# Half of batch 1's first scores inside the values of batch 0, and projections between scores

## What is computed

```python
def _layernorm(x, axis=-1, eps=1e-05): ...      # mean, variance over the last axis

# attention: x (8, 256, 512), ctx (8, 256, 512), H = 32 query heads, G = 8 key groups, head width 16
q = X @ Wq.T + bq;  k = encoder_output @ Wk.T + bk;  v = encoder_output @ Wv.T + bv
scores = jnp.einsum('bgrqd,bgkd->bgrqk', q, k) / jnp.sqrt(jnp.float32(HD))
scores = jnp.where(causal_mask..., -jnp.inf, scores); scores = jnp.where(padding_mask..., -jnp.inf, scores)
w = jax.nn.softmax(scores, axis=-1)
out = jnp.einsum('bgrqk,bgkd->bgrqd', w, v)     # then out @ Wo.T + bo

# feed-forward (512 -> 2048 -> 512), weights rounded to -1, 0, 1, activations to 8 bits
bitlinear158(x, w, b) = act_quant(rms_norm(x)) @ weight_quant(w).T + b
h = jax.nn.silu(bitlinear158(x, w1, b1)); h = jax.nn.gelu(h, approximate=False)
h = layer_norm(h, ln_g, ln_b); ffn = bitlinear158(h, w2, b2)

x = x + attention(_layernorm(x), ctx);  x = x + ffn(_layernorm(x))
```

## Time and profile before

| | |
|---|---|
| median of 3 runs | 582.51 us (580.14 to 583.58) |
| profiled execution | 581.34 us, span 579.3 us |
| busy, of the span | PE 90%, PEld 49%, DVE 85%, ACT 61%, POOL 24% |
| granted clock of PE, mean | 0.964 of full speed |
| DMA | 72.17 MB, mean 125 GB/s |
| chain that ended last | PE 54%, DVE 20%, issue 8%, DMA 7%, ACT 7% |

### The profile page before, as it was taken

The page is one execution under the profiler, slowest core; times in us unless marked ns, Lnnn a source line. Parts: engine busy times, 40 slices in busy tenths (PEclk is TensorE's granted clock), DMA queues, the critical chain, the costliest instruction groups (busy, mean ns, idle before and its releaser), DMA issues.

```text
span 579.3 us, 9027 instructions
## 1 busy us (share of the span) xinstructions
PE 520.6 (90%) x3425; PEld 285.6 (49%) x3425; DVE 491.1 (85%) x730; ACT 351.4 (61%) x424; POOL 139.9 (24%) x106
## 2 busy tenths in 40 slices
PE   4978788999899999899999999999949999798796
PEld 3856335544564557445663566445514553243343
DVE  4689929789989788988999789978896889959996
ACT  2235470687848764785659573866368576876931
POOL 5103034003410621025200611211122105133130
PEclk9986899999899999999999999999969999988999
DMA  6888595887126712463137502571115411110002
GB/s 200 277 209 317 174 279 156 335 304 170 37 66 197 163 43 79 160 179 86 72 117 183 117 16 98 161 170 40 43 39 140 101 40 42 27 30 1 36 2 75
DMA packets 32994, 72.17 MB, mean 125 GB/s; under 512 B 7167, under 2 KB 14529, under 8 KB 29950
## 3 DMA queue, kind: packets, MB, share of 16 engines
q1 hardware_dynamic: 31286, 67.13, 39.6%
q0 software_dynamic: 576, 4.19, 1.8%
q10 hardware_dynamic: 1088, 0.24, 0.2%
HBM read 46.50 MB, written 20.61 MB: 116 GB/s over the span
## 4 chain that ended last, share of the span: by engine, by line
PE 54%; DVE 20%; issue 8%; DMA 7%; ACT 7%; POOL 2%; SPq 2%; ACTq 0%; DVEq 0%
PE FF L891 8%; PE FF L943 6%; DVE negm L1416 5%; PE S L773 5%; PE PV L813 5%; ACT PT L1136 5%; PE PV L830 4%; PE S L797 4%; PE FF L710 3%; DMA num<-o_raw 2%; PE PV L773 2%; PE FF L893 2%; DVE work L1565 2%; POOL st L510 2%; PE FF L905 2%
## 5 line engine op out<-in xcount | busy, mean ns | idle before, releaser
L1136 ACT ACTIVATE PT<-S 128x1024 f32<-128x1024 f32 x128 | 123.4, 1032 | 24.0 <-PE S L797 23.6
L1416 DVE TENSOR_REDUCE negm<-S 128x4 f32<-128x1024 f32 x88 | 105.6, 1215 | 17.9 <-PE S L773 16.5
L797 PE MATMUL S<-Q,K 100*128 100x512 bf16 x256 | 73.7, 393 | 18.6 <-ACT PT L1136 14.9
L891 PE MATMUL FF<-w1t,xqT 128*128 128x512 bf16 x256 | 68.4, 390 | 5.0 <-ACT wq_sb L1170 3.4
L813 PE MATMUL PV<-PT,vaug 128*32 128x256 f32 x1024 | 70.5, 394 | 0.6 <-ACT PT L1136 0.6
L773 PE MATMUL S<-K,Q 97*128 97x256 bf16 x352 | 55.5, 284 | 5.4 <-DVE negm L1416 3.5
L830 PE MATMUL PV<-wo_sb,num 128*128 128x512 f32 x128 | 59.1, 608 | 0.0
L1170 ACT ACTIVATE work<-FF,s 128x512 f32<-128x512 f32 x48 | 33.0, 687 | 36.3 <-PE FF L893 36.3
L1416 DVE TENSOR_REDUCE negm<-PV 128x4 f32<-128x1024 f32 x40 | 48.8, 1220 | 5.6 <-PE PV L773 5.2
L710 PE MATMUL FF<-xnT,wq_sb 128*128 128x256 f32 x224 | 50.6, 381 | 0.2 <-ACT xnT L1103 0.2
L1194 ACT ACTIVATE work<-work 128x2048 bf16<-128x2048 f32 x12 | 22.9, 1911 | 45.2 <-DVE work L1571 45.0
(11 more groups left out here) (231 smaller groups left out, 905.2 us busy)
## 6 DMA issues: line engine op xcount, KB each, us to landing
Q<-q_d SPq DMA_DIRECT2D x15, 768.0 KB
q_d<-part SPq DMA_DIRECT2D x8, 768.0 KB, 3.6
x_sb<-in_x SPq DMA_DIRECT2D x8, 512.0 KB, 4.1
ctx_sb<-in_ctxT SPq DMA_DIRECT2D x8, 512.0 KB, 4.6
work<-in_w SPq DMA_DIRECT2D x4, 1024.0 KB, 13.2
q_d<-part SPq DMA_DIRECT2D x8, 512.0 KB, 3.3
xb_sb<-in_x SPq DMA_DIRECT2D x8, 512.0 KB, 4.3
work<-in_w POOLq DMA_DIRECT2D x4, 1024.0 KB, 8.9
```

Of the source, the lines that this page charges most:

```text
L797: last = pe.matmul(where, K[0:ROWS_2, g, kt * P:(kt + 1) * P], Q[0:ROWS_2, g, 2 * pair:2 * pair + 2, :], start=not masked, stop=True)
L891: pe.matmul(FF[:, n % 2, :], xqT[:, k, t * P:(t + 1) * P], w1t[:, k, cols], start=(k == 0), stop=False)
L1136: act.activation(PT[:, n % PT_SLOTS, :, :], ST[n % 2][:], ACT.Exp, scale=0.25).then_inc(S["pt_made"], 1)
L1416: dve.tensor_reduce(negm[:, t, R * g:R * g + R], RING_1[n % 3][:], AX.X, ALU.max, negate=True).then_inc(S["max_made"], 1)
```

## The change

Q and K rows of groups 0 to 3 of batch 1 get tiles of their own, `Q_first` and `K_first`, which lie in the later homes of the layer rows (`g_bc`, `b_bc`). `rows_back_own` fills them at the end of the start. The first scores of these groups run in iteration 0 as 16 half tiles of 2 matmuls (`half_scores`, banks of FF in turn), between `scores_2` and `values` from pair 3 on, with 16 maxima of 128 x 512 (`half_maximum`); the loop of full tiles is left with 8 to 15. The context of batch 1 has its own tile, so that it loads early. V of batches 0 and 1 is projected after score tiles 2 and 4 of batch 0. PE makes 11 f32 matmuls on ones before its first projection. Q pieces 2 and 3 of batch 3 move from the scores of iteration 0 to the head of iteration 1. `turn_x` and Q of batch 4 move from the head of iteration 2 to the first score tiles 10 to 15 of iteration 1, and DVE's `query_rests(4)` ahead of `gain` and `shift` in iteration 2. The output bias moves to tiles 8 to 11, the reciprocal of batch 0 behind the maximum of tile 12, the last pass over w1 and the statistics of x of batch 3 behind the half maxima. `second_weights` stands behind `divide` of batch 0 on POOL, and ACT sums w2 after all of Q of batch 3. The layer rows load behind the second half of batch 2's rows; the last bias stays where it was.

```diff
...
+        ctx_first = xb_sb[:].rearrange("p t n -> p (t n)").rearrange("p (k t) -> p k t", k=KD)
+        def ctx_of(a):
+            return ctx_first if a == 1 else ctx_sb[:, :, :]
+        def v_place(a):
+            return FFw[:, 512 * a:512 * a + 256] if a < 2 else FFw[:, 512:768]
+        Q_first = g_bc[:].bitcast(BF16).rearrange("p (g r t) -> p g r t", g=G // 2, r=R)
+        K_first = b_bc[:].bitcast(BF16)[:, 0:G // 2 * T].rearrange("p (g t) -> p g t", g=G // 2)
+        def Q_of(b, g):
+            return Q_first[:, g, :, :] if b == 1 and g < G // 2 else Q[:, g, :, :]
+        def K_of(b, g):
+            return K_first[:, g, :] if b == 1 and g < G // 2 else K[:, g, :]
+        def ring_of(a, n):
+            return RING_1[(n + 1) % 3 if a == 1 else n % 3]
...
             def load_context(a):
-                wait_for(sp, S["kv_ps"], a)
-                sp.dma_start(ctx_sb[:], ctxT[a]).then_inc(S["ctx_in"], 16)
+                if a > 1:
+                    sp.wait_ge(S["kv_ps"], a)
+                sp.dma_start(ctx_of(a), ctxT[a]).then_inc(S["ctx_in"], 16)
             def load_residual(c):
+                if at_start(c):
+                    sp.wait_ge(S["kv_ps"], 2)
                 wait_for(sp, S["x1_made"], 2 * c)
...
+            def rows_back_own():
...
+                sp.wait_ge(S["c_row"], 4)
+                sp.wait_ge(S["s1_ps"], 5)
+                gs = slice(0, G // 2)
+                sp.dma_start(Q_first[0:ROWS_SPLIT, :, :, :].rearrange("d g r t -> d (g r t)"),
+                             q_d[1][:, gs, :].rearrange("d g n -> d (g n)")).then_inc(S["rows_in0"], 16)
+                sp.dma_start(K_first[0:ROWS_SPLIT, :, :].rearrange("d g t -> d (g t)"),
+                             k_d[1][:, gs, :].rearrange("d g n -> d (g n)")).then_inc(S["rows_in0"], 16)
+                sp.dma_start(K_first[ROW_MASK:ROW_MASK + 1, :, :].rearrange("p g t -> p (g t)"),
+                             neg_d[1:2, 0:4 * T]).then_inc(S["rows_in0"], 16)
...
+            def last_bias():
+                sp.dma_start(b2_bc[:], b2.partition_broadcast(P)).then_inc(S["w_bo"], 16)
             def layer_rows():
-                for to, of in ((b2_bc, b2), (g_bc, ln_g), (b_bc, ln_b)):
+                for to, of in ((g_bc, ln_g), (b_bc, ln_b)):
                     sp.dma_start(to[:], of.partition_broadcast(P)).then_inc(S["w_two"], 16)
...
                 if at_start(f):
-                    layer_rows()
+                    last_bias()
...
-                if a is not None:
+                if a is not None and a > 1:
                     rows_back(a, 0)
...
                 if a is not None:
                     rows_back(a, 1)
+                if at_start(f):
+                    layer_rows()
                 if c is not None:
                     denominators(c, 3)
                     numerators(c, 1)
...
+                if c is not None:
+                    divide(c)
                 if at_start(c):
                     second_weights()
-                if c is not None:
-                    divide(c)
...
-                if a > 3:
+                if a == 4:
+                    pe.wait_ge(S["silu_made"], 8)
...
             def project_v(a):
-                if a == 1:
-                    pe.wait_ge(S["v_placed"], 1)
-                to = pair_of(a)
+                if a == 0:
+                    pe.wait_ge(S["q_made"], 4)
+                    pe.wait_ge(S["r1q_made"], 4)
+                to = v_place(a)
...
+                since = n - 8 if a == 1 else n
+                if since < 2:
+                    wait_for(pe, S["pt_made"], 16 * (a - 1) + 15 + since)
+                elif since == 2:
...
-                to = RING_1[n % 3]
+                to = ring_of(a, n)
...
+            def half_scores(h, masked):
...
+                if h > 1 and pair == 0:
+                    pe.wait_ge(S["max_half"], h // 2)
+                elif h > 1:
+                    pe.wait_ge(S["max_made"], 16 + h // 2)
+                to = FF[:, pair, :].rearrange("p (r t) -> p r t", r=2)
...
+                              start=True, stop=False)
+                for r in range(2):
+                    last = pe.matmul(to[:, r, :], Q_first[0:ROWS_1, g, 2 * pair + r, t * P:(t + 1) * P],
+                                     K_first[0:ROWS_1, g, :], start=not masked, stop=True)
+                last.then_inc(S["s1_half" if pair == 0 else "s1_ps"], 1)
...
             def body_of(c, a, f, t, masked):
-                w = next_front(a) if c > 1 else None
+                w = next_front(a) if c > 2 else None
                 if w is not None:
                     turn_x(w)
                 if f is not None and not at_start(f):
                     project_out(f, 0, c)
                 turn_max(c)
                 if at_start(f):
+                    project_q(3, (2, 3))
                     project_out(f, 0, c)
...
+                    if at_start(c) and 3 <= g < G:
+                        half_scores(3 * g - 9, masked)
                     if c is not None and g > 0:
                         values(c, 2 * g - 2)
+                        if at_start(c) and 3 <= g:
+                            half_scores(3 * g - 9 + (g < G), masked)
                         values(c, 2 * g - 1)
+                        if at_start(c) and 3 <= g < G:
+                            half_scores(3 * g - 7, masked)
...
-                for n in range(16):
+                for n in range(8 if at_start(c) else 0, 16):
                     if a is not None:
                         scores_1(a, n, masked)
                     if at_start(c):
-                        if 1 <= n <= 4:
-                            output_bias(n - 1)
-                        if n == 8:
+                        if 8 <= n <= 10:
+                            output_bias(n - 8)
+                        if n == 10:
+                            output_bias(3)
+                        if n == 12:
                             turn_x(3)
-                        if n in (10, 12, 14, 15):
-                            project_q(3, ((10, 12, 14, 15).index(n),))
+                        if 13 <= n <= 14:
+                            project_q(3, (n - 13,))
+                    if at_start(f):
+                        if n == 10:
+                            turn_x(4)
+                        if n >= 12:
+                            project_q(4, (n - 12,))
                     if f is not None and n < 8:
                         layer_1(f, n, t)
...
                     scores_1(0, n, masked)
+                    if n in (2, 4):
+                        project_v(n // 2 - 1)
...
+            pe.wait_ge(S["c_ones"], 1)
+            for _ in range(11):
+                pe.matmul(PV[:, 0, 0:P], ones[:], ones[:], start=True, stop=True)
             project_k(0)
             turn_x(0)
-            project_v(0)
             project_q(0)
...
+                if c == 1 and n == 0:
+                    act.wait_ge(S["w_abs"], 8)
...
+                    weight_abs_sum(0, (0,))
+                    values_in(0)
                     values_in(1)
-                    weight_abs_sum(0, (0, 1, 2))
+                    weight_abs_sum(0, (1, 2))
...
-                w = next_front(a) if c != 1 else None
+                w = next_front(a) if c not in (1, 2) else None
...
                 if at_start(c):
                     turned_x(3)
                     queries(3, 0)
-                    weight_abs_sum(1, (0, 1))
                     queries(3, 1)
-                    weight_abs_sum(1, (2, 3))
...
                 if f is not None:
                     for n in range(8):
                         silu(f, n)
+                    if at_start(f):
+                        turned_x(4)
                     gelu(f, 0)
+                    if at_start(f):
+                        queries(4, 0)
                     gelu(f, 1)
                     deviations(f, 0)
+                    if at_start(f):
+                        queries(4, 1)
                     deviations(f, 1)
...
+            def half_maximum(h):
+                g, t, pair = h // 4, h // 2 % TT, h % 2
+                if pair == 0:
+                    dve.wait_ge(S["s1_half"], h // 2 + 1)
+                else:
+                    dve.wait_ge(S["s1_ps"], 16 + h // 2 + 1)
+                dve.tensor_reduce(negm[:, t, R * g + 2 * pair:R * g + 2 * pair + 2],
+                                  FF[:, pair, :].rearrange("p (r t) -> p r t", r=2), AX.X, ALU.max, negate=True
+                                  ).then_inc(S["max_half" if pair == 0 else "max_made"], 1)
...
-                if t is not None:
+                if t is not None and not at_start(t):
                     spread_3(t)
                     gain(t, 0)
                 if at_start(c):
@@ -1774,8 +1892,11 @@
                     max_rows(c)
                 if at_start(c):
                     weight_scale(0)
-                if at_start(f):
+                if at_start(f) or at_start(t):
```

(12 more changed lines are left out.)

90 lines of the change are left out of this document (56 added, 34 removed).

## The result

The changed kernel takes 601.7 us (median of 4 runs, 601.25 to 604.07), the kernel before 582.2 us in the same series. The ratio is 1.034, with a 95% interval of 1.030 to 1.037: 19.5 us slower. The forecast was 596 us, with a range of 584 to 603.

A forecast was written before the change was run, and what follows sets the result against it. The limit was taken to change by stage, PE having half of the chain and DVE a fifth. Parts 1 to 5 end in +3.4 and the others add 10.0: +13.4 on 581.3, 594.7, stated as 596 us, range 584 to 603.

The forecast's parts named there:

- the case that was given 0.60: The main forecast for the whole kernel: 596 us, its own range 590 to 601, chance 0.60.
- Part 1: Start: warm-up matmuls halve the first projection's time and V of batch 0 leaves; -2.4 us, bounds -0.5 to -2.4.
- Part 2: Iteration 0: batch 1's rows, issued on SP just ahead of batch 0's maxima write, delay it; +0.7 us, 0 to 2.4.
- Part 3: Values of iteration 0: three half tiles per pair lengthen PE's period to 2.6 us; +1.9 us, bounds 0 to +3.3.
- Part 4: Remaining full score tiles of batch 1: eight maxima less, partly offset by later transposes and two Q pieces; -5.0 us.
- Part 5: Head of iteration 1: w2 issued late, first exponential 21.0 us behind the last maximum, at +3.4 instead of -4.7 us.
- Part 6: Iteration 1: PE waits some 4 us, so values run at a lower clock; +0.7 us, range 0 to 2.1.
- Parts 7 and 8: Iteration 1: batch 4's x and Q between score tiles, +1.3 us; layer rows on the queue delay denominators and reciprocal, +2.5 us.
- Part 9: Head of iteration 2: DVE's rests come first, first exponential 22.6 to 22.8 us behind the last maximum, not 19.4; +3.4 us.
- Part 10: Iteration 2: PE, early through its shortened head, runs the values at a lower clock; +2.1 us, bounds 0 to 2.1.
- The half tiles do not overlap: Rival: in iteration 0 each half tile waits for the maximum two back, losing most of the full-tile gain; 601, chance 0.08.
- Worse: queues at their upper ends: Rival: late w2 +5.6, cold values of iteration 1 +2.1, layer rows delaying denominators +4.1; 602 us, chance 0.12.

The follow-up runs named there:

- start_three: Changed kernel with batch 1's constant-row fills later on GpSimd, 17 warm-up products instead of 11, and batch 1's own rows fetched behind the maxima's write and read: 598.5 us.
- no_half_tiles: Changed kernel with batch 1's first scores as 16 full tiles behind batch 0's values again, and what belongs to them as before: 593.0 us, ratio 1.015.
- w2_early: Changed kernel with batch 0's reciprocal behind tile 9, w2's transfer ahead of the division, two w2 sums ahead of batch 3's second Q pair: 602.1 us.
- rows_late: Changed kernel with the layer rows issued behind the last denominators, numerators and the reciprocals' transfers: 600.5 us, ratio 1.030.
- dve_order: Changed kernel with VectorE's order of before in iteration 2, first gain early and rests of batch 4's Q behind the second shift: 601.9 us, ratio 1.033.
- q3_piece_up: Changed kernel with the third piece of batch 3's Q moved behind the last score tile of batch 1: 603.8 us, ratio 1.035.
- before_v: Kernel before with only V of batches 0 and 1 put between the first scores: 580.9 us, ratio 0.999.
- before_v_warm: Kernel before with V of batches 0 and 1 between the first scores and 17 warm-up products: 581.1 us, ratio 0.997.

## Why the prediction was right, and where it was not

The direction, the range and the sum of the later parts held. But 601.7 lies 1.3 us below the upper end of the range, and above the 590 to 601 of the case that was given 0.60. From batch 1's first exponential to the end it is 469.7 us, 460.2 before: +9.5, forecast +10.0. Up to there it is +10.5, forecast +3.4, and that is the miss. Of its signs, those of the first half failed (first projection at half its duration, last maximum near 101.5, DMA waits ahead of the sums over w2, exponential near 122.5), and those of the second half came (reciprocal waiting for a DMA, 22 to 23 us, clock at 0.50).

- **Part 1, start -2.4: wrong, +0.5.** The step "If the 11 matmuls raise the clock before the weights land" failed: they ended 2.6 us too soon. 17 of them gave 1.8 us. That the memsets on POOL cost nothing failed too: 1.85 us of VectorE, for which TensorE waited 1.04. In start_three, with the fill later, the two instructions take 1.00 us again. By the Trainium skill ("SBUF — State Buffer", Who interferes with whom) a VectorE tensor_scalar in a two-port mode and a GpSimd instruction exclude each other for a whole instruction; the trace agrees in size, 1.80 us of fill and 1.00 of work making 2.85, and does not show the mode.
- **Part 2, rows ahead of the maxima +0.7:** +1.0, and start_three shows that the rows cause it.
- **Part 3, half tiles +1.9:** +3.3. The term was mis-sized: each pair became 2.87 us, not 2.6. Three half tiles are six matmuls, and the row it cites, 1.05 us for eight, gives 0.79 us and not 0.65; in the trace they hold TensorE for 0.87 us of each pair (0.32 us from the start of one to the values behind it, 0.23 to the scores). That the first pairs ran cold adds little: it happened before too, and the fourth pair starts 8.3 us behind the first exponential, 8.0 before.
- **Part 4, the remaining full tiles -5.0: wrong, +0.3.** From the last exponential's end to the last maximum it is 23.4 us, 23.1 before. The term failed in its second half. The first full maximum comes 5.9 us behind the last exponential's end, forecast 5.1 (90.1 on the forecast's clock). From there to the last maximum's end it is 17.5 us, forecast 13.1, and VectorE idles 6.7 of them: 2.4 behind the output bias, which the forecast gave no time of its own, and 4.3 behind the Q pieces, priced at 1.7, the first of which took 3.50 us at the lower clock. Eight tiles no longer cover the work that sixteen did. no_half_tiles shows parts 3 to 5 together at 9.4 us; how part 4 splits was only read from the trace.
- **Part 5, w2 late:** the wrong bound. It put 21.0 us between last maximum and exponential where 18.4 were measured. w2 was issued 0.6 us behind the maximum, not 2.4, and TensorE's queue, which the text had at 16.4, set the exponential (w2_early). It took 18.4 because the two Q pieces, priced at 3.6 us, took 5.36 with the clock down, and 0.5 more came from `divide` beside the split. By luck this wrong bound hid 2.6 us of part 4's miss. w2 is the next bound, 2 us below.
- **Part 6, cold values in iteration 1 +0.7:** 0; TensorE did not wait there.
- **Parts 7 and 8, +1.3 and +2.5:** +1.7 and +3.0 (rows_late), with the cause as given. By the Trainium skill ("DMA: Bandwidth & Descriptors", Queues, rings and completion order) each DMA engine takes descriptors in the order of its ring; the trace agrees: with the layer rows behind them the denominators are no longer waited for.
- **Part 9, iteration 2 +3.4:** 22.6 us behind the last maximum, as forecast (22.6 to 22.8), a difference of +3.1 to a head that was itself 1.4 us slow. But the reason, VectorE's order, is only half of it: dve_order has the same 22.5 us through K.
- **Part 10, cold values +2.1:** +1.6.

Of the rivals, "The half tiles do not overlap" gives 601, close to what was measured, and the loss of part 4's gain. Its mechanism did not occur: in the trace no half tile waits for a maximum. "Worse: queues at their upper ends" gives 602 and did not occur either, since no sum over w2 waited.

## What to carry to other kernels

Work moved into another stage's gaps must be checked against what stood in the stage that it leaves: eight maxima fewer saved nothing here, and by the trace the reason is that the output bias, transposes and projections that had run beside them then kept VectorE waiting. An earlier start is kept only if the next transfer is earlier too, and a TensorE that had waited 2.7 to 4.0 us came back at half clock in q3_piece_up, before_v and before_v_warm. Whatever is moved on GpSimd has to be looked up beside VectorE's short operations too. Where two chains end within 2 us of each other, shortening one can show nothing until the other is shortened too.

## What the runs showed of the hardware

- With 0.72 and 0.61 us of TensorE work in two windows of 2 us the granted clock fell to 0.50 in q3_piece_up; in the changed kernel it stayed at 1.00 through nearly the same gap (0.94 and 0.80 us). 2.4 us of the difference between the two stretches, which have the same code, lie behind this point.
- A fill of four partitions on GpSimd (1.80 us) lengthened two VectorE instructions on other data from 1.00 to 2.85 us.
- An operation of 128x64 on VectorE took 0.20 us alone and up to 2.25 us beside a GpSimd multiplication of 2.34 us on other data; in eight kernels it ended within 0.1 us of it.
- A small write of maxima took 1.5, 3.4 or 4.1 us to its read's issue, depending on whether 0.96 MB was issued 4.1, 1.6 or 0.7 us ahead of it.
